# Products of the second layer's weights: from the end of the scatter to the waits behind feed-forward and query projections

## The chip, the cores and the metric

One core of one Trainium2 chip runs the whole program. The metric is the device time in microseconds of one execution. Inputs lie in the chip's memory when it starts. Inputs, weights and output are float32.

## The reference, cut to what matters

Two layers of a network on 1250 nodes with 512 features and 40,000 edges. Each layer adds a graph part and a mixing part to x and then a feed-forward part. The graph part of the first layer is attention over edges, and the second layer's is a graph convolution with two weights in a row:

```python
xn = _layernorm(x, axis=-1)
x = x + _L0_gnn_ref(xn, ...) + _L0_mix_ref(xn[None], ...)[0]
x = x + _L0_ffn_ref(_layernorm(x, axis=-1)[None], ...)[0]
xn = _layernorm(x, axis=-1)
x = x + _L1_gnn_ref(xn, edge_index, W_gcn, b_gcn, W_dense, b_dense) + _L1_mix_ref(xn[None], w_qkv, ..., w_q, w_k)[0]
x = x + _L1_ffn_ref(_layernorm(x, axis=-1)[None], w_q, keys, weight_down_embed, weight_up_embed)[0]

# L1_gnn:  agg = segment_sum(h[src] * norm) + b_gcn, h = embedding @ W_gcn;   return agg @ W_dense + b_dense
# L1_mix:  q, k, v from w_qkv;  alpha = softmax(einsum(q, w_q));  ...
# L1_ffn:  q = x @ w_q / sqrt(1 + eps);  h = einsum('bnd,bnhkd->bnhk', q, weights_down)
```

Three products of weights alone can be formed ahead of layer 2, and the kernel does: W_gcn W_dense with the bias b_gcn W_dense + b_dense + b_proj (`wgd`, `l1_bias`), the query weights times w_q by head (`aq`), and the last part's w_q times the 256 rows of weight_down that can be chosen (`wqd`).

## The kernel before, in words

The program is written by hand, engine by engine. The end of the kernel calls the stages of each engine one after the other (L2555 to L2610); the engines meet at the stage ends in `leave_stage` (L140: TensorE, ScalarE and VectorE each drain, count up `s_stage` and wait until all three have). Rows of nodes are worked on in 10 tiles of 125. SBUF is one tensor `arena`, in which each stage lays out its buffers by hand with `Space`, and PSUM is one tensor `banks` of 8 banks. A float32 matmul stands in the trace as two records.

Stages of layer 0, in order: edges, mix, gnn, att, ff, ffn, causal, expert. Beside edges, mix and gnn, GpSimd scatters the edges' weights into a table in memory of 1250 x 1250 cells with 9 numbers each (`edges_pool`, indirect DMAs at L503): 313 columns of 128 edges. A column is issued when the one before the last has landed (`s_scat`), and its values must have been summed by VectorE (`s_group`).

The stages that the change touches:

- `gnn_*` (L894 to L1101): attention's query, key and value projections, then the row maxima of the scores (L1071, reduced by VectorE at L961), then the shifts, transposed by TensorE (L1077) and copied by ScalarE (L1007, to `shiftT`). Behind these stands the folding of the weights: VectorE spreads `w_q` on a diagonal (L969 to L971), TensorE multiplies (`fold_part` L1083, biases L1091 and L1092), ScalarE copies the banks out (L1013, L1014), SyncE stores and loads the next pair of weights (L909), TensorE multiplies again (L1083, L1099), ScalarE copies (L1016, L1017) and SyncE stores (L914, L915). The handshake is one semaphore, `f_step`.
- `att_*` (L1168 on): attention over a table block of 125 x 250 cells at a time, 50 of them. SyncE first loads Wo, waits for the stage's end, loads W1, waits until all columns of the scatter have landed (`table_filled`, L507) and then loads three blocks, each in two transfers (L203, L204). ScalarE begins a block at L1277, and takes exponentials at L1280. A ring of three buffers holds the blocks.
- `ff_*`: feed-forward part. TensorE's matmuls at L1479 and in `project` (L189), VectorE adds the result at L1423 and takes statistics (L157) for the next layer norm.
- `ffn_*`: VectorE makes two layer norms in a row (L146 to L177); TensorE transposes z (L183), ScalarE copies it out as zT (L1581), TensorE projects on q, k and v (L189), VectorE copies (L1548). Then ScalarE squares (L1590), VectorE sums (L1552), a root (L1593) and norms follow, and TensorE transposes q and k (L183, copied at L1597).
- `l1_sp` loads the folded weights at 1904 us, when the expert stage starts (`s_fold`).

SyncE's queue is in the order of the program: a DMA that stands behind a wait goes out after it, whatever it is for.

```python
            sp.wait_ge(s_sum, TURNS)                  # L901, in gnn_sp
        def att_sp(sp):
            sp.dma_start(wo_g..., d["L0_gnn_Wo"])     # L1169
            sp.wait_ge(s_stage, 6)
            sp.dma_start(w1_most, ...)                # L1171
            table_filled(sp)
```

## Time and profile before

| what | before |
|---|---|
| runs, median (lowest to highest) | 2730.16 us (2728.12 to 2730.72), 3 runs |
| the profiled execution, its own time | 2739.05 us |
| its span, first to last instruction | 2737.3 us |
| mean granted TensorE clock | 0.911 |
| TensorE busy | 2327.8 us (85%) |
| VectorE busy | 1388.9 us (51%) |
| ScalarE busy | 737.6 us (27%) |
| GpSimd busy | 813.4 us (30%) |
| chain that ended last | TensorE 65%, VectorE 23%, ScalarE 5%, GpSimd 3%, issue 3%, DMA 1% |

How to read it: busy is the time in which an engine had an instruction of its own under way. The chain goes back from the last instruction, each step to what released it. PE is TensorE's matmul, PEld its weight loads, DVE is VectorE, ACT ScalarE, POOL GpSimd, SP SyncE, and a q behind a name is that engine's own queue. A granted clock of 1.00 is 2.4 GHz, 0.50 is 1.2 GHz. All starts are in us from the span's start.

### The profile page before, as it was taken

The page shows a single profiled execution, that of the slowest core. Times are in us where ns is not written, and L with a number is a line of the kernel's source. Part 1 is how long each engine was busy: PE and PEld are TensorE (multiplying, and loading weights), DVE is VectorE, ACT ScalarE, POOL GpSimd, SP SyncE. Part 2 cuts the span into 40 slices and gives each one's busy share as a digit, 9 for nine tenths or more (in the row PEclk, how much of TensorE's full clock was granted, in tenths as well). Part 3 has the DMA queues.
Part 4 walks back from the last instruction along what each step waited for, and adds up shares of the span by engine and source line. Part 5 has one row for each costly group of instructions (what it writes and reads, how often), then busy time and mean ns, then how long its engine had stood idle before and what let it go on. Part 6 is the DMA issues. An engine that isn't in the chain of part 4 may idle for free.

```text
span 2737.3 us, 30781 instructions
## 1 busy us (share of the span) xinstructions
PE 2327.8 (85%) x11164; PEld 1358.4 (50%) x11164; DVE 1388.9 (51%) x4120; ACT 737.6 (27%) x1583; POOL 813.4 (30%) x532
## 2 busy tenths in 40 slices
PE   1999895998968999988969588998999989988863
PEld 0455452443334444446634467777866733444431
DVE  4555666779906656641132533230122242499996
ACT  3111021220005444432211544442211110144432
POOL 2038887887836655530000000000000000012221
PEclk9997777998979999989989799996999999989977
DMA  9972222223248656640000200001100040000000
GB/s 347 418 283 3 3 3 18 4 4 41 3 116 207 169 156 167 164 139 1 1 0 0 93 1 1 1 1 65 60 1 1 1 111 16 0 1 9 10 8 11
DMA packets 90264, 180.59 MB, mean 66 GB/s; under 512 B 65109, under 2 KB 66070, under 8 KB 74135
## 3 DMA queue, kind: packets, MB, share of 16 engines
q1 hardware_dynamic: 44367, 176.77, 20.1%
q0 software_dynamic: 45072, 1.46, 5.1%
q8 instruction: 89, 1.46, 0.2%
q14 instruction: 62, 0.51, 0.1%
q10 hardware_dynamic: 674, 0.39, 0.1%
HBM read 110.27 MB, written 68.31 MB: 65 GB/s over the span
## 4 chain that ended last, share of the span: by engine, by line
PE 65%; DVE 23%; ACT 5%; POOL 3%; issue 3%; DMA 1%; SPq 0%; ACTq 0%; DVEq 0%; POOLq 0%
PE banks L189 19%; PE banks L1940 5%; PE banks L1967 5%; DVE arena L961 4%; PE banks L1769 4%; PE banks L1788 4%; PE banks L325 3%; PE banks L1479 3%; PE banks L1303 3%; PE banks L183 2%; PE banks L1316 2%; PE banks L1778 2%; PE banks L1803 2%; POOL arena L1260 2%; DVE arena L1228 1%
## 5 line engine op out<-in xcount | busy, mean ns | idle before, releaser
L189 PE MATMUL banks<-arena 128*125 128x512 f32 (+1 forms) x1280 | 602.9, 620 | 84.3 <-ACT arena L2444 74.9
L503 POOL DMA_INDIRECT edge_table<-arena x313 | 490.8, 1568 | 256.4 <-DMA edge_table<-arena 165.0
L189 PEld LDWEIGHTS banks<-arena 128*125 128x125 f32 x1280 | 245.6, 201 | 375.7 <-issue 279.5
L1228 DVE TENSOR_TENSOR arena<-banks,arena 125x500 f32<-125x500 f32 x200 | 208.6, 1051 | 180.0 <-ACT banks L1280 176.3
L1260 POOL TENSOR_TENSOR arena<-arena 125x500 f32<-125x500 f32 x180 | 222.5, 1245 | 173.1 <-DVE arena L1228 167.4
L2278 POOL MEMSET arena<- 128x1024 f32 x2 | 1.8, 951 | 675.0 <-DVEq L140 675.0
L183 PE MATMUL banks<-arena 125*128 125x125 f32 x600 | 101.5, 309 | 105.9 <-DVE arena L177 69.9
L1682 DVE CUSTOM_DVE_ANT_0 arena<-banks,arena 125x512 f32<-125x512 f32 (+8 forms) x144 | 74.9, 554 | 212.2 <-PE banks L1778 209.7
L1303 PE MATMUL banks<-arena 64*125 64x250 f32 x800 | 142.6, 434 | 36.9 <-DVE arena L1228 25.8
L1888 DVE SCALAR_TENSOR_TENSOR arena<-banks,arena 125x512 f32<-125x512 f32 x80 | 60.1, 751 | 203.7 <-PE banks L1967 203.7
L183 PEld LDWEIGHTS banks<-arena 125*128 125x128 f32 x600 | 76.6, 160 | 170.4 <-issue 94.2
L1280 ACT ACTIVATE banks<-banks 125x500 f32<-125x500 f32 x200 | 114.6, 573 | 172.5 <-PE banks L1306 172.1
L1940 PEld LDWEIGHTS banks<-arena 128*128 128x128 f32 x1280 | 144.5, 193 | 6.9 <-issue 6.8
L1940 PE MATMUL banks<-arena 128*128 128x125 f32 x1280 | 146.2, 276 | 0.0
L1967 PE MATMUL banks<-arena 128*125 128x512 f32 x320 | 139.1, 592 | 0.0
L1769 PE MATMUL banks<-arena 128*125 128x512 f32 (+10 forms) x288 | 117.9, 531 | 22.3 <-ACT arena L1719 22.3
L1316 PE MATMUL banks<-arena 125*64 125x250 f32 x800 | 130.8, 406 | 0.9 <-ACT arena L1266 0.7
L1071 PE MATMUL banks<-arena 64*125 64x512 f32 (+1 forms) x480 | 113.7, 578 | 6.0 <-DVE arena L961 4.7
L325 PE MATMUL banks<-arena 1*128 1x512 f32 x160 | 99.7, 706 | 20.5 <-DMA arena<-key_rows 12.8
L334 ACT ACTIVATE arena<-banks 128x512 f32<-128x512 f32 x80 | 47.8, 598 | 254.9 <-PE banks L325 249.7
L1303 PEld LDWEIGHTS banks<-arena 64*125 64x125 f32 x800 | 61.0, 187 | 109.9 <-DVE arena L1228 69.9
L1788 PE MATMUL banks<-arena 125*125 125x64 f32 x880 | 113.7, 281 | 1.5 <-ACT arena L1750 1.5
(314 smaller groups left out, 3621.1 us busy)
## 6 DMA issues: line engine op xcount, KB each, us to landing
edge_table<-arena SPq DMA_DIRECT2D x24, 2250.0 KB, 36.2
arena<-edge_table SPq DMA_DIRECT2D x50, 984.4 KB
arena<-L_ffn_W SPq DMA_DIRECT2D x4, 2048.0 KB, 8.4
arena<-edge_table SPq DMA_DIRECT2D x50, 114.3 KB
adjacency<-arena SPq DMA_DIRECT2D x50, 109.4 KB
arena<-adjacency SPq DMA_DIRECT2D x10, 546.9 KB
edge_table<-arena POOLq DMA_INDIRECT x313, 3.0
arena<-x SPq DMA_DIRECT2D x1, 2240.0 KB
```

The lines of the kernel that those rows point to most:

```text
L183: last = nc.tensor.transpose(dst[:, k, :], src[:, k * 128:(k + 1) * 128], ident[0:TP, 0:TP])
L189: last = nc.tensor.matmul(dst, xT[:, i, :], w[:, i, 0:n], start=(i == 0), stop=(i == k - 1))
L325: nc.tensor.matmul(line_bank(h), ones[p:p + 1, 0:EP], line[p:p + 1, :], start=True, stop=True).then_inc(s_wide, 1)
L503: pool.indirect_dma_start(d["table"], bass.IndirectOffsetOnAxis(ap=cell[0:EP, c:c + 1].bitcast(U32), axis=0), vals[0:EP, c * ROW:(c + 1) * ...
L1228: nc.vector.tensor_tensor(P_g[n % PRING][0:TP, :].rearrange("p (e n) -> p e n", e=2), two_scores(n), ring[(c * TILES + b) % RING][0:TP, :, ...
L1260: nc.gpsimd.tensor_tensor(total_p, P_g[(n - PAIRS) % PRING][0:TP, :] if b == 1 else total_p, P_g[n % PRING][0:TP, :], ALU.add).then_inc(a_ ...
L1303: nc.tensor.matmul(bank(at + e)[0:TP, 0:CHUNK], kT_g[64 * e:64 * e + 64, j, tok(b)], qT_g[64 * e:64 * e + 64, j, sources(c)], start=True, ...
L1316: last = nc.tensor.matmul(bank(j // 2)[64 * e:64 * e + 64, CHUNK * (j % 2):CHUNK * (j % 2 + 1)], V_g[0:TP, b, DH * (2 * j + e):DH * (2 * j ...
L1769: nc.tensor.matmul(bank(score_bank(s, j))[0:TP, 0:c1 - c0], qz_c[:, h, :], kT_f[:, h // 2, c0:c1], start=True, stop=True).then_inc(b_s, 1)
L1788: last = nc.tensor.matmul(bank(6)[0:TP, h * DH:(h + 1) * DH], pTc_v[0:TP, b, :], V_f[0:TP, b, h * DH:(h + 1) * DH], start=(b == 0), stop=( ...
L1940: last = nc.tensor.matmul(bank(2 + n % 3)[:, m * TP:(m + 1) * TP], w1_e[a // 2][:, k, (c % 8) * 128:(c % 8 + 1) * 128], yT[:, k, tok(t)], ...
L1967: last = nc.tensor.matmul(bank(5 + n % 3)[0:TP, :], hT_e[t % 2][:, 2 * e + c, :], w2_e[e // 4][:, 2 * (e % 4) + c, :], start=(c == 0), sto ...
```

## The change

The fold's work stays the same, instruction by instruction, apart from where it stands:

- The SyncE part, `fold_sp`, is called between `ffn_sp` and `expert_sp`. The first weights are loaded behind the projections' weights, at the start of feed-forward. Of the second pair `wqT` is loaded only when the first products have been stored (`s_fold` 32), since its buffer holds them.
- `fold_dve` is the last thing of `ff_dve`. Attention on VectorE no longer waits for `s_fold`.
- TensorE's first products (`fold_dense_pe`) are the first thing of `ffn_pe`, in banks 4 to 7 with the bias row in bank 3. ScalarE copies them out (`fold_dense_act`) behind its first zT, and TensorE waits for this before its second projection (bank 3).
- The second products (`fold_query_pe`, banks 5 to 7) stand behind the projections, and ScalarE copies them (`fold_query_act`) behind the root.
- The buffers lie at the end of the arena; products overwrite the weights that they were made from.

```diff
@@ -861,9 +861,6 @@
-        both_bias = kept_g.take(C)
-        wq_col, bg_col = kept_g.take(KC), kept_g.take(KC)
-        wq_diag = kept_g.take(KC * HEADS).rearrange("p (k h) -> p k h", h=HEADS)
@@ -875,11 +872,16 @@
-        fold = Space(3 * SLOT, 4 * SLOT)
-        left_w, right_w = chunks(fold.take(KC * C), C), chunks(fold.take(KC * C), C)
-        down_w = chunks(fold.take(KC * KEYS), KEYS)
-        fold = Space(BUF, BUF + 4616)
-        wgd_out, bias_out, aq_out, wqd_out = (fold.take(n) for n in (KC * C, C, KC * HEADS, KC * KEYS))
+        fold = Space(BUF + 4064, TOP)
+        both_bias = fold.take(C)
...
+        fold = Space(TOP - 2 * KC * C - KC * KEYS, TOP)
+        right_w, down_w = chunks(fold.take(KC * C), C), chunks(fold.take(KC * KEYS), KEYS)
+        left_w = chunks(fold.take(KC * C), C)
+        wgd_out, bias_out = right_w, both_bias
...
@@ -899,20 +901,6 @@
             sp.wait_ge(s_sum, TURNS)
-            for w, n in ((left_w, "L1_gnn_W_gcnT"), (right_w, "L1_gnn_W_dense"), (down_w, "L1_ffn_down")):
...
-            sp.wait_ge(f_step, 5)
-            sp.dma_start(d["aq"], aq_out).then_inc(s_fold, 16)
-            sp.dma_start(d["wqd"], wqd_out).then_inc(s_fold, 16)
@@ -1193,7 +1146,6 @@
         def att_dve(dve):
-            dve.wait_ge(s_fold, 16 * 4)
@@ -1426,6 +1378,7 @@
             dve.wait_ge(f_x, TILES)
+            fold_dve(dve)
             leave_stage(dve, "DVE")
@@ -1524,6 +1477,67 @@
+        def fold_sp(sp):
+            for w, n in ((left_w, "L1_gnn_W_gcnT"), (right_w, "L1_gnn_W_dense"), (down_w, "L1_ffn_down")):
+                sp.dma_start(w.rearrange("p k n -> p (k n)"), d[n]).then_inc(s_fw[0], 16)
...
+            sp.wait_ge(f_step, 2)
+            sp.dma_start(left_w.rearrange("p k n -> p (k n)"), d["L1_mix_WqT"]).then_inc(s_fw[1], 16)
+            sp.wait_ge(f_step, 3)
+            sp.dma_start(d["wgd"], wgd_out.rearrange("p k n -> p (k n)")).then_inc(s_fold, 16)
+            sp.dma_start(d["l1_bias"], bias_out[0:1, :]).then_inc(s_fold, 16)
+            sp.wait_ge(s_fold, 32)
+            sp.dma_start(right_w.rearrange("p k n -> p (k n)"), d["L1_ffn_wqT"]).then_inc(s_fw[1], 16)
+            sp.wait_ge(f_step, 5)
+            sp.dma_start(d["aq"], aq_out).then_inc(s_fold, 16)
+            sp.dma_start(d["wqd"], wqd_out).then_inc(s_fold, 16)
+
+        def fold_dve(dve):
+            dve.wait_ge(s_fw[0], 16 * 6)
+            link(dve, nc.vector.memset(wq_diag, 0.0))
...
+        def fold_dense_pe(pe):
+            pe.wait_ge(f_step, 1)
+            for m in range(KC):
+                fold_part(bank(4 + m), m, right_w)
+            for k in range(KC):
+                nc.tensor.matmul(bank(3)[0:1, :], bg_col[:, k:k + 1], right_w[:, k, :], start=(k == 0), stop=False)
...
+        def fold_dense_act(act):
+            act.wait_ge(f_step, 2)
+            for m in range(KC):
+                nc.scalar.activation(wgd_out[:, m, :], bank(4 + m), ACT.Copy)
+            nc.scalar.activation(bias_out[0:1, :], bank(3)[0:1, :], ACT.Copy).then_inc(f_step, 1)
+
+        def fold_query_pe(pe):
+            pe.wait_ge(s_fw[1], 32)
...
+        def fold_query_act(act):
+            act.wait_ge(f_step, 4)
...
@@ -1582,6 +1596,8 @@
                 last.then_inc(z_cols, 1)
+                if t == 0:
+                    fold_dense_act(act)
@@ -1591,6 +1607,7 @@
             nc.scalar.activation(sa[0:TP, :], sv[0:TP, :], ACT.Sqrt).then_inc(c_sr, 1)
+            fold_query_act(act)
@@ -1599,6 +1616,7 @@
         def ffn_pe(pe):
+            fold_dense_pe(pe)
             pe.wait_ge(s_wc, 16 * 8)
@@ -1613,10 +1631,13 @@
+                    if t == 0 and j == 1:
+                        pe.wait_ge(f_step, 3)
                     project(bank(2 + j)[0:TP, :], zT_c[t % 2], w).then_inc(c_proj, 1)
...
             pe.wait_ge(c_ev, 3 * TILES)
+            fold_query_pe(pe)
@@ -2563,6 +2584,7 @@
             ffn_sp(sp)
+            fold_sp(sp)
             expert_sp(sp)

```

How the order moves on SyncE, at the end of the gnn stage and the begin of attention (`fold_step` is `f_step`, `repeats_summed` is `s_sum`, `stage_left` is `s_stage`, `columns_scattered` is `s_scat`). Before:

```order
L909 DMA arena<-L_mix_WqT 128x2048 [waits fold_step]
L909 DMA arena<-L_ffn_wqT 128x2048
L911 DMA gcn_dense_weights<-arena 128x2048 [waits fold_step]
L912 DMA l_bias<-arena 1x512
L914 DMA global_query_weights<-arena 128x32 [waits fold_step]
L915 DMA expert_down_weights<-arena 128x1024
L1169 DMA arena<-L_gnn_Wo 128x2048
L1171 DMA arena<-L_gnn_W 128x3072 [waits stage_left]
L1172 DMA arena<-L_gnn_W 128x1024
L203 DMA arena<-edge_table 112x2250 [waits columns_scattered_1,columns_scattered_0]
L204 DMA arena<-edge_table 13x2250
L203 DMA arena<-edge_table 112x2250
```

The same place now, from the wait for `s_sum` on:

```order
L196 DMA arena<-L_gnn_ln_att_b 128x4
L1122 DMA arena<-L_gnn_Wo 128x2048 [waits repeats_summed]
L1124 DMA arena<-L_gnn_W 128x3072 [waits stage_left]
L1125 DMA arena<-L_gnn_W 128x1024
L203 DMA arena<-edge_table 112x2250 [waits columns_scattered_1,columns_scattered_0]
L204 DMA arena<-edge_table 13x2250
L203 DMA arena<-edge_table 112x2250
L204 DMA arena<-edge_table 13x2250
```

Wo's load follows the wait for `s_sum`, W1's the end of the stage, and no fold transfer is among them. They stand behind the projections' weights now:

```order
L196 DMA arena<-L_ffn_kn_g 128x1
L1482 DMA arena<-L_gnn_W_gcnT 128x2048
L1482 DMA arena<-L_gnn_W_dense 128x2048
L1482 DMA arena<-L_ffn_down 128x1024
L1483 DMA arena<-L_bias_rows 2x512
L1484 DMA arena<-L_mix_w_q 128x4
L1485 DMA arena<-L_gnn_b_gcn 128x4
L1487 DMA arena<-L_mix_WqT 128x2048 [waits fold_step]
L1489 DMA gcn_dense_weights<-arena 128x2048 [waits fold_step]
L1490 DMA l_bias<-arena 1x512
L1492 DMA arena<-L_ffn_wqT 128x2048 [waits folded_weights_stored]
L1494 DMA global_query_weights<-arena 128x32 [waits fold_step]
L1495 DMA expert_down_weights<-arena 128x1024
```

TensorE between feed-forward (last rows with 125x512 of it) and the projections, before:

```order
L189 MATMUL banks<-arena 125x512 x7
L183 MATMUL banks<-arena 128x125 [waits z_ready,ffn_qkv_weights_loaded,stage_left]
L183 MATMUL banks<-arena 128x125 x3
L189 MATMUL banks<-arena 125x512 [waits zT_ready]
L189 MATMUL banks<-arena 125x512 x3
L183 MATMUL banks<-arena 128x125 [waits z_ready]
L183 MATMUL banks<-arena 128x125 x3
L189 MATMUL banks<-arena 125x512 x8
```

And now:

```order
L189 MATMUL banks<-arena 125x512 x7
L1506 MATMUL banks<-arena 128x512 [waits fold_step,stage_left]
L1506 MATMUL banks<-arena 128x512 x15
L1515 MATMUL banks<-arena 1x512 x4
L1516 MATMUL banks<-arena 1x512
L183 MATMUL banks<-arena 128x125 [waits z_ready,ffn_qkv_weights_loaded]
L183 MATMUL banks<-arena 128x125 x3
L189 MATMUL banks<-arena 125x512 [waits zT_ready]
L189 MATMUL banks<-arena 125x512 x3
L183 MATMUL banks<-arena 128x125 [waits z_ready]
L183 MATMUL banks<-arena 128x125 x3
L189 MATMUL banks<-arena 125x512 [waits fold_step]
L189 MATMUL banks<-arena 125x512 x7
```

The 21 fold matmuls stand ahead of the first transposes, and the second projection has a wait for the copies.

## Rows read from the trace of the kernel before

**Rows 1.** Chain that ended last, 600 to 860 us: start us, us, what.

```profile
760.33 15.56 PE banks L1083 x32
...
780.76 8.73 DMA arena<-L_ffn_wqT
789.54 7.00 PE banks L1083 x32
796.53 9.50 PE banks L1099 x32
...
810.48 14.41 DMA arena<-edge_table
```

**Rows 2.** Timeline, SyncE queue: start us, us, engine line op out<-in.

```profile
780.39 0.33 SPq L909 DMA_DIRECT2D arena<-L_mix_WqT  x1
...
809.34 0.47 SPq L1172 DMA_DIRECT2D arena<-L_gnn_W  x1
809.92 0.50 SPq L203 DMA_DIRECT2D arena<-edge_table  x1
```

**Rows 3.** Timeline, ScalarE: in brackets idle time before and who ended it.

```profile
760.43 3.10 ACT L1007 ACTIVATE arena<-banks 8x500 bf16<-8x500 f32 x6 [128.37 <-PE banks L1077]
```

**Rows 4.** Timeline, GpSimd: columns of the scatter.

```profile
639.12 1.86 POOL L503 DMA_INDIRECT edge_table<-arena  x1 [2.02 <-DMA edge_table<-arena]
644.50 1.54 POOL L503 DMA_INDIRECT edge_table<-arena  x1 [3.52 <-DMA edge_table<-arena]
...
781.80 1.54 POOL L503 DMA_INDIRECT edge_table<-arena  x1 [0.30 <-issue]
790.60 1.54 POOL L503 DMA_INDIRECT edge_table<-arena  x1 [7.26 <-DMA edge_table<-arena]
```

**Rows 5.** One line, L503: time from a column's issue to its landing.

```profile
DMA to landing us min/median/max: 2.9/3.0/11.5
```

**Rows 6.** Chain that ended last, from feed-forward into the projections.

```profile
1380.62 0.60 DVE arena L157
...
1402.42 5.25 PE banks L189 x8
...
1408.10 10.30 PE banks L189 x24
```

**Rows 7.** Timeline, TensorE, first transposes of the projections.

```profile
1399.71 1.06 PE L183 MATMUL banks<-arena 125*128 125x125 f32 x4 [19.90 <-DVE arena L177]
```

**Rows 8.** Windows of 1 us: busy time by engine, then TensorE's granted clock, DMA share, GB/s.

```profile
1384.00:1385.00 1.00, 0.00 (x0) 0.00 (x0) 0.24 (x2) 0.62 (x2) 0.00 (x0) 1.00 0.00 0
1385.00:1386.00 1.00, 0.00 (x0) 0.00 (x0) 0.86 (x5) 0.00 (x0) 0.00 (x0) 0.55 0.00 0
1386.00:1387.00 1.00, 0.00 (x0) 0.00 (x0) 1.00 (x3) 0.00 (x0) 0.00 (x0) 0.50 0.00 0
```

**Rows 9.** Groups by line, 1511 to 1531 us: TensorE behind the projections.

```profile
L183 PE MATMUL banks<-arena 125*128 125x125 f32 x3 | 0.9, 424 | 19.3 <-DVE arena L1568 19.3
```

**Rows 10.** Timeline, SyncE queue, inside attention: one table block.

```profile
834.71 0.34 SPq L203 DMA_DIRECT2D arena<-edge_table  x1
```

**Rows 11.** Windows of 0.5 us, columns as in rows 8.

```profile
840.00:840.50 0.50, 0.50 (x6) 0.13 (x6) 0.00 (x0) 0.50 (x3) 0.46 (x1) 1.00 0.02 1
```

**Rows 12.** DMA issues by line, KB and median us to landing: W1's last part.

```profile
arena<-L_gnn_W SPq DMA_DIRECT2D x1, 512.0 KB, 10.9
```

**Rows 13.** Timeline, VectorE: the fold's memset and its last copy.

```profile
757.98 0.09 DVE L969 MEMSET arena<- 128x32 f32 x1
...
758.28 0.45 DVE L971 COPY arena<-arena 64x4 f32<-64x4 f32 x1
```

**Rows 14.** Timeline, ScalarE: copies of the first products.

```profile
780.39 2.06 ACT L1013 ACTIVATE arena<-banks 128x512 f32<-128x512 f32 x4 [16.87 <-PE banks L1092]
```

**Rows 15.** Timeline, ScalarE: the root behind the projections.

```profile
1526.60 0.34 ACT L1593 ACTIVATE arena<-arena 125x160 f32<-125x160 f32 x1 [1.03 <-DVE arena L1556]
```

**Rows 16.** Groups by line, 805 to 1210 us: ScalarE's first work on each table block.

```profile
L1277 ACT ACTIVATE arena<-arena 125x250 f32<-125x250 f32 x50 | 32.5, 650 | 17.8 <-DMA arena<-edge_table 17.8
```

More of the change, by code:

```diff
@@ L1010, in gnn_act @@
             last.then_inc(g_shift, 1)
-            act.wait_ge(f_step, 2)
-            for m in range(KC):
-                nc.scalar.activation(wgd_out[:, m * C:(m + 1) * C], bank(3 + m), ACT.Copy)
-            nc.scalar.activation(bias_out[0:1, :], bank(7)[0:1, :], ACT.Copy).then_inc(f_step, 1)
-            act.wait_ge(f_step, 4)
-            nc.scalar.activation(aq_out, bank(3)[:, 0:KC * HEADS], ACT.Copy)
-            nc.scalar.activation(wqd_out, banks[:, 4 * BANK:6 * BANK], ACT.Copy,
-                                 scale=1.0 / (1.0 + 1e-5) ** 0.5).then_inc(f_step, 1)
             leave_stage(act, "ACT")
@@ new lines, in fold_dve, with fold_part @@
+        def fold_dve(dve):
+            dve.wait_ge(s_fw[0], 16 * 6)
+            link(dve, nc.vector.memset(wq_diag, 0.0))
+            nc.vector.tensor_copy(wq_diag.rearrange("p k h -> p (k h)")[0:64, 0:KC * HEADS:10], wq_col[0:64, :])
+            nc.vector.tensor_copy(wq_diag.rearrange("p k h -> p (k h)")[64:128, 1:KC * HEADS:10],
+                                  wq_col[64:128, :]).then_inc(f_step, 1)
+        def fold_part(dst, m, right):
+            for k in range(KC):
+                last = nc.tensor.matmul(dst, left_w[:, k, m * 128:(m + 1) * 128], right[:, k, :],
+                                        start=(k == 0), stop=(k == KC - 1))
+            return last
@@ new lines, in fold_dense_pe @@
+        def fold_dense_pe(pe):
+            pe.wait_ge(f_step, 1)
+            for m in range(KC):
+                fold_part(bank(4 + m), m, right_w)
+            for k in range(KC):
+                nc.tensor.matmul(bank(3)[0:1, :], bg_col[:, k:k + 1], right_w[:, k, :], start=(k == 0), stop=False)
+            nc.tensor.matmul(bank(3)[0:1, :], ones[0:2, 0:1], both_bias[0:2, :], start=False, stop=True).then_inc(f_step, 1)
+        def fold_dense_act(act):
[3 more added lines that the diff above has]
+            nc.scalar.activation(bias_out[0:1, :], bank(3)[0:1, :], ACT.Copy).then_inc(f_step, 1)
@@ new lines, in fold_query_pe @@
+        def fold_query_pe(pe):
+            pe.wait_ge(s_fw[1], 32)
+            for m in range(KC):
+                fold_part(bank(5)[:, m * HEADS:(m + 1) * HEADS], m, wq_diag)
+            for m in range(KC):
+                for k in range(KC):
+                    last = nc.tensor.matmul(bank(6 + m // 2)[:, KEYS * (m % 2):KEYS * (m % 2 + 1)],
+                                            right_w[:, k, m * 128:(m + 1) * 128], down_w[:, k, :],
+                                            start=(k == 0), stop=(k == KC - 1))
+            last.then_inc(f_step, 1)
```

46 lines of the change are left out of this document (10 added, 36 removed).

## The prediction

> **What bounds the kernel now.** I read the chain of work that ended last first, around the place that the change empties. From 760.3 us it runs over TensorE's products of the second layer's weights, then the load of L1_ffn_wqT, then more products, and then 14.4 us of a table load, with which attention begins [rows 1]. So the folding stage itself bounds that stretch, and nothing of it is needed before layer 2. The question is what is next in line once it is gone. The SyncE queue says that: it issued L1_mix_WqT at 780.39, and the first W1 load and table block only at 809.3 and 809.9, after the last fold product [rows 2]. ScalarE, whose copies of the shifts are the last thing that the stage would have without the fold, started those at 760.43 and needed 3.1 us, so the stage could be left at about 763.8 [rows 3]. What is then late is the scatter on GpSimd: its 313th and last column was issued at 790.60, after a wait of 7.26 us for an earlier column's transfer [rows 4]. A column normally lands 3.0 us after its issue, and at worst 11.5 [rows 5]. The waits stand where SyncE moves megabytes: 2.02 and 3.52 us at 639 and 644, behind 2.5 MB of fold weights, and 7.26 us at 783 to 790, behind 2 MB of loads and 1 MB of stores. Elsewhere a column follows its predecessor after 0.30 us.
>
> Then I read the two places that take the work in. Between feed-forward and query projections TensorE stands idle for 19.9 us, and then it does its first four matmuls of the projections (8 records) in 5.25 us, where later ones take 10.30 us for 24 [rows 6, 7]: its granted clock had fallen from 1.00 to 0.55 and then 0.50 by 1386 [rows 8], that is from 2.4 to 1.2 GHz, after some 5 us without work. Behind the projections it stands idle for 19.3 us more [rows 9].
>
> **The change, part by part.**
>
> *The end of the scatter.* Three transfers change on SyncE while columns are under way. (a) At 635 us the queue issues W_gcnT, W_dense and down, 2.5 MB, and now only the 1 MB of L0_gnn_Wo. The stall of 2.02 + 3.52 - 2 x 0.30 = 4.94 us shrinks in proportion to 40%, so 3.0 us are saved. The ends are 0 (the stall comes from any load) and 4.94. (b) At about 763.8 the 2 MB of L0_gnn_W1 now start, beside the scatter: 4.94 x 2/2.5 = 4.0 us of new stall. The ends are 0 and 6.96, the stall of the larger burst. (c) The burst at 780 goes: 7.26 - 0.30 = 6.96 us saved [rows 4]. The last column is then issued at 790.60 - 3.0 + 4.0 - 6.96 = 784.6 and lands at 787.6.
>
> One rule of the Trainium skill speaks of (a) to (c). "DMA: Bandwidth & Descriptors", section "Queues, rings and completion order", says that a DMA engine goes round the queues that have work, a packet from each at a time. By that a column waits for a packet and not for megabytes, and (b) would cost nothing. The trace speaks against it with its 7.26 us.
>
> *The first table block.* It is now issued when the last column has landed, and nothing is ahead of it. The nearest row is a single block in the middle of attention: issued at 834.71, with the DMA engines quiet from 840.0, which is 5.3 us [rows 10, 11]. The other end is what block 0 took before, from 809.92 to 824.97 = 15.1 us, with 3 MB of Wo and W1 ahead and two blocks behind; of these W1's last part landed 10.9 us after its issue, at 820.2, and block 0 only 4.7 us later [rows 2, 12]. I take 6.5 us: the single block and a little for the two blocks queued behind it. Attention then begins at 787.6 + 6.5 = 794.1 instead of 824.97. This is **30.9 us** sooner. From there on it runs as before.
>
> *Between feed-forward and projections.* VectorE gets the memset and two copies of the diagonal weights, on the path, since its layer norm follows: from 757.98 to 758.73 = **0.75 us** [rows 13]. TensorE gets 16 + 4 + 1 matmuls, 42 records. At full clock 512 columns take 10.30 / 24 = 0.43 us a record [rows 6], so 18.0 us. It can begin when VectorE has left the stage, at 1380.62 + 0.60 + 0.75 = 1382.0, and the first transpose of the projections is ready at 1399.71 + 0.75 = 1400.5. That is 18.4 us of cover for 18.0 us of work. It just fits, and if the cover were gone each further microsecond would be late. The clock should stay up, because the gap before the fold is 2.2 us and the clock fell only after 5. So transposes and first projection find it high: four transposes take about 0.65 instead of 1.08 us, and eight records 3.44 instead of 5.25, together 2.2 us won. ScalarE copies five banks out behind its first zT, 4 x 512 columns in 2.06 us and a fifth of 0.5, 2.6 us in all [rows 14]; TensorE needs those banks only after 3.44 + 0.43 us of other work, so this costs nothing. The sum here is 0.75 - 2.2 = **-1.5 us**. The loads that this needs, 2.5 MB behind the projections' weights, are issued at the start of feed-forward, over 150 us before they are waited for.
>
> The second rule is on the clock. "TensorE: Matmul & The Clock Gate", section "HAM oscillation — how this bites in real kernels", says that work broken up by waits may drop to the lower clock again each time. It would put the gaps around the fold at 1.2 GHz and take the 2.2 us away. Which it is, no row of before shows for this pattern.
>
> *Behind the projections.* 32 more matmuls took 7.00 + 9.50 = 16.5 us before, part of it at half clock [rows 1]. They lie in the 19.3 us in which VectorE and ScalarE form the norms [rows 9]. ScalarE's two copies, together some 1.2 us by that same rate, come behind its root at 1526.60 [rows 15] and before the first transposed tile that it waits for, some 4 us later. The chain of transfers in between (WqT in, products out, wqT in) has over 100 us. This costs nothing. If the cover failed, only what exceeds 19.3 us would show. The stores of the products are needed in layer 2 only.
>
> *Sum.* -30.9 - 1.5 = -32.4 us. The profiled execution took 2739.05 us, so 2706.7 of its kind. The median of the runs, 2730.16, lies 8.9 us lower, and the same step from there gives **2698 us** (2697.8).
>
> **The rivals.**
>
> *Table blocks stay slow.* The 15.1 us of block 0 came from the three blocks that share the engines and not from the 3 MB ahead. For it: all three are issued within 3 us, and nothing says that the first of them is served first. Against it: 4.7 us after W1 sufficed [rows 2, 12]. Attention begins 8.6 us later than I say, so 2706.4.
>
> *Columns are hardly disturbed by W1.* That is the mechanism of a fair share between the queues, under which (b) costs nothing. The last column lands 4.0 us earlier: 2693.8, and with the 5.3 us of a single block 2692.6. For it: W1 is two transfers, where the burst at 635 was six, of which any may have been the one in the way. Against it: the stall at 783 to 790, behind two loads and a store [rows 4]. It is the round-robin of the rule cited above.
>
> *The fold outlives its cover.* The clock falls before or in the fold, and 42 records at twice 0.43 us take 36 us: 17.7 us late. Then the gain of 2.2 us is gone too, and -30.9 + 0.75 + 17.7 = -12.5 gives 2717.7. Against it: the short gap, and the matmuls stand without a wait among them.
>
> *Attention becomes bound by its table loads.* This is the one that ends slower. Attention begins with block 0 alone in memory, and blocks 1 and 2 still on their way, so it runs closer behind its loads. Before, ScalarE waited for a table block 17.8 us in all 50, all of it at the first [rows 16]. If the loads set the pace and each of the 50 blocks took over 32.4 / 50 = 0.65 us longer, all would be lost; at 0.8 us it is 40 - 32.4 = 7.6 us slower, 2737.8. Against it: a single block took 5.3 us, and the engines were then quiet.
>
> *Nothing moves.* Something else than the fold holds attention until 825. The chain and the queue's order leave little room for that: 2730.
>
> **How the numbers follow.** Forecast 0.62; slow table blocks 0.14; undisturbed columns 0.12; fold outlives its cover 0.06; attention bound by its loads 0.03; nothing moves 0.03. The forecast's own spread is 2694 to 2703, by the ends of (a), (b) and of the 2.2 us. The range takes in the cases on both sides of it, down to 2690 (no stall by W1 and the whole 4.94 us at 639 saved) and up to 2708. A measurement of this kernel can tell some 0.2%, 5.5 us, from no change. Faster by more than that are the first four cases and most of a spread around them, 0.94; same 0.03; slower 0.03.
>
> **What would show it.** In the profile after, the last GpSimd column should be issued near 784.6 (780 to 788) with stalls at 637 of 1 to 3 us and new ones of about 4 us just behind 764; the first exponential's chain should start near 794. The chain should show GpSimd's issues and no product between 760 and 790. The 42 fold records should start some 2 us behind the last feed-forward matmul and take 18 us, the granted clock should stay 1.00 until the projections, and ScalarE's copies should keep no one. The query products should end before the transposes. I am wrong if the last column comes at 790 again, if block 0 needs over 9 us, or if TensorE shows the fold still running when the first transposed rows are ready. A chain that passes through table loads later in attention would mean the rival that ends slower.

## The result, and the profile after

| what | before | after |
|---|---|---|
| runs in one job, median (lowest to highest) | 2729.32 us (2728.12 to 2730.72), 4 runs | 2712.84 us (2708.07 to 2715.86), 4 runs |
| ratio of after to before | | 0.9938, interval 0.9921 to 0.9955 |
| profiled execution / its span | 2739.05 / 2737.3 us | 2713.70 / 2712.0 us |
| mean granted TensorE clock | 0.911 | 0.914 |

Faster by 0.6%, or 16.5 us. The forecast was 2698 us and its range ended at 2708. In a second job the kernel after, unaltered, had 2708.69 us, at a ratio of 0.9915 (0.9902 to 0.9928).

The two profiled executions lie 25.3 us apart in their spans. The chain of work that ended last, in the profile after, from 600 to 860 us (start us, us, what), answers to [rows 1]:

```profile
629.51 5.94 DMA edge_table<-arena
635.72 2.98 POOL edge_table L503
...
758.02 8.57 DMA edge_table<-arena
...
791.10 2.94 DMA edge_table<-arena
794.44 6.59 DMA arena<-edge_table
```

There is no product between 760 and 790 any more; the chain is the scatter, column by column, and then the first table block. Its columns in the timeline of GpSimd answer to [rows 4], and the SyncE queue to [rows 2]:

```profile
631.42 1.87 POOL L503 DMA_INDIRECT edge_table<-arena  x1 [0.36 <-DVE arena L425]
635.72 2.98 POOL L503 DMA_INDIRECT edge_table<-arena  x1 [2.44 <-DMA edge_table<-arena]
639.01 1.67 POOL L503 DMA_INDIRECT edge_table<-arena  x1 [0.30 <-issue]
...
766.86 1.54 POOL L503 DMA_INDIRECT edge_table<-arena  x1 [5.46 <-DMA edge_table<-arena]
...
791.10 1.54 POOL L503 DMA_INDIRECT edge_table<-arena  x1 [0.42 <-issue]
```

```profile
630.36 0.33 SPq L1122 DMA_DIRECT2D arena<-L_gnn_Wo  x1
758.90 0.33 SPq L1124 DMA_DIRECT2D arena<-L_gnn_W  x1
...
794.06 0.34 SPq L203 DMA_DIRECT2D arena<-edge_table  x1
794.44 0.41 SPq L204 DMA_DIRECT2D arena<-edge_table  x1
```

The stall behind 780 is gone, and the one of W1 is there, just behind 759, as forecast. But the last column is issued at 791.10, where the forecast had 784.6. ScalarE starts its first block 10.0 us behind that (first line). Its copy of the last block starts at 1160.32 (second line); before, it started at 1185.69 (L1285):

```profile
801.11 0.65 ACT L1229 ACTIVATE arena<-arena 125x250 f32<-125x250 f32 x1 [42.27 <-DMA arena<-edge_table]
...
1160.32 0.38 ACT L1237 ACTIVATE arena<-banks 125x250 f32<-125x250 f32 x1 [0.41 <-PE banks L1280]
```

Between feed-forward and projections TensorE's timeline now reads as follows; it answers to [rows 6, 7]. The last two are the first products of q, k, v, and what follows on them:

```profile
1356.37 13.97 PE L1506 MATMUL banks<-arena 128*128 128x512 f32 x32 [1.97 <-DVEq L140]
1370.27 3.59 PE L1515 MATMUL banks<-arena 128*1 128x512 f32 x8
1373.80 1.01 PE L1516 MATMUL banks<-arena 2*1 2x512 f32 x2
1374.74 0.65 PE L183 MATMUL banks<-arena 125*128 125x125 f32 x4
1377.03 5.21 PE L189 MATMUL banks<-arena 128*125 128x512 f32 x8 [1.65 <-ACT arena L1595]
...
1382.51 7.89 PE L189 MATMUL banks<-arena 128*125 128x512 f32 x18
```

The 42 records of the fold run at full clock, take 18.4 us and end just when the first transposes can begin. The windows behind it (columns as in [rows 8]) show the granted clock falling from 1.00 to 0.50, thus from 2.4 to 1.2 GHz, in a gap of 1.65 us behind the transposes:

```profile
1375.00:1376.00 1.00, 0.39 (x4) 0.15 (x2) 0.55 (x1) 0.51 (x2) 0.00 (x0) 1.00 0.41 49
1376.00:1377.00 1.00, 0.00 (x0) 0.00 (x0) 0.00 (x0) 1.00 (x4) 0.00 (x0) 0.85 0.58 164
1377.00:1378.00 1.00, 0.97 (x1) 0.50 (x2) 0.00 (x0) 1.00 (x3) 0.00 (x0) 0.50 1.00 426
```

Behind the projections the query products lie in the wait, with 4.34 us to spare [rows 9]:

```profile
1490.74 9.83 PE L1530 MATMUL banks<-arena 128*128 128x256 f32 x32
1504.91 5.27 PE L183 MATMUL banks<-arena 125*128 125x125 f32 x25 [4.34 <-DVE arena L1582]
```

### The profile page after: what moved, and what is told of

Its sections match the earlier page's. It is cut to its first block, busy times and chain, and to the rows that moved or that the text cites. A ratio compares the mean times of both kernels' runs of the same rounds, so it can differ in the third digit from the quotient of the medians.

```text
span 2712.0 us, 30781 instructions
## 1 busy us (share of the span) xinstructions
PE 2316.4 (85%) x11164; PEld 1349.5 (50%) x11164; DVE 1390.1 (51%) x4120; ACT 737.7 (27%) x1583; POOL 818.3 (30%) x532
## 4 chain that ended last, share of the span: by engine, by line
PE 47%; POOL 18%; DVE 14%; issue 6%; DMA 5%; SPq 5%; ACT 4%; DVEq 0%; ACTq 0%; POOLq 0%
POOL edge_table L503 15%; PE banks L189 9%; PE banks L1961 5%; DMA edge_table<-arena 5%; PE banks L1988 5%; SPq L293 4%; PE banks L1790 4%; PE banks L1809 4%; PE banks L1432 3%; PE banks L1255 3%; PE banks L1268 2%; PE banks L1799 2%; PE banks L1824 2%; POOL arena L1212 2%; DVE arena L1180 1%
## 5 line engine op out<-in xcount | busy, mean ns | idle before, releaser
L503 POOL DMA_INDIRECT edge_table<-arena x313 | 495.7, 1584 | 252.3 <-DMA edge_table<-arena 161.3
```

The lines of the kernel that those rows point to most:

```text
L503: pool.indirect_dma_start(d["table"], bass.IndirectOffsetOnAxis(ap=cell[0:EP, c:c + 1].bitcast(U32), axis=0), vals[0:EP, c * ROW:(c + 1) * ...
```

## The experiments

All profiles are read by four lengths: when the last column is issued; from there to ScalarE's first block; attention, from that to ScalarE's copy of the last block; and the rest of the span.

| profile | last column | to first block | attention | rest | span |
|---|---|---|---|---|---|
| before | 790.60 | 34.37 | 360.72 | 1551.6 | 2737.3 |
| before_again | 787.68 | 32.37 | 358.65 | 1551.6 | 2730.3 |
| before_no_adds | 790.64 | 21.22 | 359.28 | 1553.6 | 2724.7 |
| after | 791.10 | 10.01 | 359.21 | 1551.7 | 2712.0 |
| a_again | 785.94 | 10.18 | 359.24 | 1551.5 | 2706.9 |
| more_load | 787.21 | 10.11 | 359.10 | 1554.9 | 2711.3 |
| adds_double | 782.65 | 10.29 | 363.02 | 1551.8 | 2707.8 |
| adds_late | 785.31 | 10.04 | 359.93 | 1550.7 | 2706.0 |
| w1_late | 776.61 | 10.30 | 363.51 | 1551.6 | 2702.0 |
| w1_wo_late | 782.70 | 9.98 | 373.03 | 1548.7 | 2714.4 |
| block0_alone | 785.04 | 9.77 | 361.55 | 1552.0 | 2708.4 |
| fill_gap | 784.67 | 9.88 | 359.49 | 1549.5 | 2703.5 |
| w1_pieces | 780.51 | 10.18 | 361.25 | 1551.8 | 2703.7 |
| best | 776.02 | 9.87 | 363.13 | 1551.8 | 2700.8 |

**The kernel after once more (a_again).**

> The changed kernel once more, unaltered. Theory (the scatter now sets when attention begins, so its stalls, which fall differently in each execution, show in the time): runs spread over some 8 us as before (2708 to 2716), the last column is issued between 786 and 794 us, and its time differs from this profile's 2713.7 by about as much as the last column differs from 791.1. Rival (the profile was a chance one and something else spreads the runs): last column within 1 us of 791.1, time elsewhere by several us.

It took 2708.69 us (2705.85 to 2710.46). The last column came 5.16 us sooner than in the first profile, and the span is 5.1 us shorter; the three other lengths agree within 0.2 us. So the kernel after follows its last column one for one. W1's stall is the same again (5.63 us at 761.76).

**W1 out of the scatter (w1_late), and Wo too (w1_wo_late).**

```diff
-            sp.dma_start(w1_most, ...)      # and w1_last, in att_sp ahead of table_filled
...
+                if i == 5:                  # behind table block 8 in attention
+                    sp.dma_start(w1_most, ...)      # w1_wo_late: Wo ahead of it, too
```

> The changed kernel with the 2 MB of L0_gnn_W1 loaded behind the sixth table block, no longer beside the scatter. Theory (megabytes on SyncE's queue hold up the scatter's columns, and the scatter bounds): no 5 us stall at about 760 us, last column some 5 us earlier (786), and 5 us less in all, 2708. Rival (queues share fairly, the stall at 766.9 was chance): last column unchanged within 2 us, 2713.

> As the run before, and the 1 MB of L0_gnn_Wo moved behind the sixth table block too. Theory: the stall of 3.6 us at 632 to 636 goes as well, last column 8 to 9 us earlier than in the changed kernel (782 to 783), 2704. Rival (one megabyte is too little to hold a column): as w1_late.

Without W1 no column waits behind 754 us; the first fence is w1_late, columns 301 to 313. In attention ScalarE then waits for a table block, which it does nowhere in the kernel after but at the first one (second fence, w1_late):

```profile
754.36 1.54 POOL L503 DMA_INDIRECT edge_table<-arena  x1 [0.30 <-issue]
...
776.61 1.54 POOL L503 DMA_INDIRECT edge_table<-arena  x1 [0.39 <-issue]
```

```profile
845.76 0.64 ACT L1230 ACTIVATE arena<-arena 125x250 f32<-125x250 f32 x1 [2.56 <-DMA arena<-edge_table]
```

Attention takes 4.3 us more, and the median is 2708.53 us (ratio 0.9924, 0.9907 to 0.994): the same as a_again. With Wo there too attention takes 373.0 us, 2710.94 us (ratio 0.9921, 0.9908 to 0.9933). W1's stall is W1's own: shown, since the four kernels without W1 beside the scatter have no such wait. What I had not expected stands in w1_wo_late. With Wo gone, the stall at 635 was still there. Its GpSimd and VectorE rows, and the window (columns as in [rows 8]) in which only 6 GB/s move:

```profile
631.48 6.11 DVE L934 TENSOR_TENSOR arena<-arena 125x512 f32<-125x512 f32 x10
632.03 1.55 POOL L503 DMA_INDIRECT edge_table<-arena  x1 [0.30 <-issue]
635.50 3.50 POOL L503 DMA_INDIRECT edge_table<-arena  x1 [1.91 <-DMA edge_table<-arena]
639.30 1.66 POOL L503 DMA_INDIRECT edge_table<-arena  x1 [0.30 <-issue]
```

```profile
630.00:635.00 5.00, 3.92 (x16) 1.92 (x18) 4.83 (x13) 0.00 (x0) 3.09 (x2) 0.50 0.28 6
```

Two columns are 3.58 us late here (start to start, beyond the usual 1.845 us), beside VectorE's ten additions of the output bias (L934 after, L946 before). These lay beside SyncE's burst in before too. The lateness has two parts. The issue at 635.50 itself took GpSimd 3.50 us instead of 1.54, and ahead of it GpSimd waited 1.91 us for a transfer. For that wait the additions are not the only candidate: at 633.2, in the same microseconds, stands a transfer of 16 KB on queue 8, of the kind that the profile calls instruction. This is the queue list of w1_wo_late from 632 to 635 us:

```profile
q0 software_dynamic: 288, 0.01, 30.9%
q8 instruction: 1, 0.02, 2.0%
```

The small pauses of the scatter go with these transfers as well. In the 14 profiles, from 250 to 755 us and leaving out the places of loads and additions and column 297 (0.7 to 0.9 us late in each), 58 columns were late by 0.7 to 1.6 us. 57 of them were issued 2.0 to 3.1 us behind the start of a 16 KB transfer of this kind. Of the 2841 columns that were on time (late by under 0.1 us), 48 were. No run moved these transfers, so that they hold the columns up is argued from this coincidence. Every profile has one beside the additions, too.

**A megabyte more (more_load).**

```diff
             sp.dma_start(w1_last, ...)
+            sp.dma_start(ring[0]..., d["L0_gnn_Wo"])      # 1 MB into a free buffer
+            sp.wait_ge(s_wo_g, 32)                       # ahead of the first table block
```

> The changed kernel with one megabyte more loaded beside the scatter at the stage's end, a copy of L0_gnn_Wo into a ring buffer that is still free (nothing reads it). Theory (a stall grows with the megabytes, 2.6 us each): stall of 7 to 8 us in place of 5.2, last column near 793.5, 2715 to 2716. Rival (a fixed stall for any burst): stall stays at 5.2, 2713.

```profile
760.65 1.54 POOL L503 DMA_INDIRECT edge_table<-arena  x1 [4.59 <-DMA edge_table<-arena]
762.97 1.54 POOL L503 DMA_INDIRECT edge_table<-arena  x1 [0.78 <-DMA edge_table<-arena]
```

The median was 2712.27 us (2705.18 to 2714.53). 3 MB cost the scatter 4.8 us in this one profile. The 2 MB of W1 cost 5.2 (after), 5.3 (a_again), 4.2 (adds_double), 5.0 (adds_late), 5.5 (block0_alone) and 4.8 us (fill_gap). From 2 to 3 MB the stall doesn't grow. It is no fixed sum either. In each of the 14 profiles SyncE loads four biases of 256 KB each at some 430 us (a_again from 429.02 on), and one column behind them is late by only 1.6 to 2.3 us:

```profile
434.14 1.54 POOL L503 DMA_INDIRECT edge_table<-arena  x1 [1.90 <-DMA edge_table<-arena]
```

The burst that the change removed, 2 MB in and 1 MB out, cost 7.0, 7.6 and 7.4 us in before, before_again and before_no_adds, each with a 16 KB instruction transfer beside it, which W1's stall did not have.

**Which of the two makes the stall at 637: loads or additions.**

```diff
 # before_no_adds (from before; it leaves the output bias out), and adds_late (from after)
-            for t in range(TILES):
-                nc.vector.tensor_tensor(XN[0:TP, t, :], XN[0:TP, t, :], bo_g[0:TP, :], ALU.add)
 # adds_late, in att_dve, its bias loaded into another place
+                if c == 0 and j == 2:
+                    nc.vector.tensor_tensor(XN[0:TP, b, :], XN[0:TP, b, :], bo_k[0:TP, :], ALU.add)
 # adds_double (from after): a wait for the end of each of the ten, and ten more behind them
-                nc.vector.tensor_tensor(XN[0:TP, t, :], XN[0:TP, t, :], bo_g[0:TP, :], ALU.add)
+                link(dve, nc.vector.tensor_tensor(XN[0:TP, t, :], XN[0:TP, t, :], bo_g[0:TP, :], ALU.add))
+            for t in range(TILES):
+                link(dve, nc.vector.tensor_tensor(z_g[0:TP, :], XN[0:TP, t, :], bo_g[0:TP, :], ALU.add))
```

> The kernel before without VectorE's ten additions of the output bias to x (it leaves them out), which lie exactly beside the stall of the scatter at 637 us, at the same moment as SyncE's 2.5 MB. Theory A (VectorE's two-operand additions in SBUF keep GpSimd from writing its descriptors; 3.6 us of the 4.9 are theirs): the stall there shrinks to 1 to 2 us. Theory B (the prediction: the megabytes make the whole stall): it stays 4.5 to 5.5 us. The time moves by no more than the stall and the 6 us of additions taken off VectorE's chain in front of the maxima.

> The kernel after with the ten additions taken out of the scatter's time: each stands in attention, one in each of the first ten table blocks, behind a product of that block. Wo's megabyte stays where it is. Theory A: no column near 630 to 640 us waits over 1 us, the scatter gains 3 to 3.6 us less what Wo's megabyte costs by itself, and VectorE leaves the stage 6 us sooner, so W1 is issued sooner. Attention takes 359.2 us as in the kernel after, or up to 3 us more if the ten additions are not hidden. Time 2704 to 2710 against 2708 to 2713 of the kernel after. Theory B: 3 to 4 us of stall remain at the load, and nothing is gained.

> The kernel after with ten further additions of the same size on VectorE behind the ten, their results thrown away, each with a wait for its end. The megabyte of Wo is loaded as before. Theory A (the additions make the stall): two to three columns are held up, in all 6 to 8 us instead of 3.6. Theory B (the load makes it): 3.6 us as now, over when the load is in. The stage's end moves by 6 to 7 us with the additions in either case, so the stall of W1 starts later too.

```profile
627.10 1.62 POOL L503 DMA_INDIRECT edge_table<-arena  x1 [0.34 <-issue]
635.36 1.54 POOL L503 DMA_INDIRECT edge_table<-arena  x1 [6.64 <-DMA edge_table<-arena]
```

These are before_no_adds. The stall is 6.4 us with no addition beside it: theory A falls for the kernel before. In adds_late one column waits 4.21 us at 636.57 with no addition beside it either, 4.0 us late. So neither load nor additions are needed for a stall, and the two don't add up:

| beside the columns at 625 to 650 us, besides 16 KB of instructions in each | columns late by |
|---|---|
| 256 KB of bias (best) | 1.5 us |
| ten additions (w1_wo_late) | 3.6 us |
| 1 MB and 256 KB of bias (adds_late) | 4.0 us |
| 1 MB and the additions (after, a_again, more_load, w1_late, block0_alone, fill_gap, w1_pieces) | 3.9, 3.9, 4.0, 4.0, 4.0, 4.4, 3.2 us |
| 2.5 MB (before_no_adds) | 6.4 us |
| 2.5 MB and the additions (before, before_again) | 5.2, 6.1 us |

Some 1.5 us of each may thus be neither of the two. What is the additions' own is the long issue: with the ten back to back, GpSimd took 2.7 to 3.8 us for one issue in seven of ten profiles. In the four others (before_no_adds, adds_late, best and adds_double) no issue here took over 1.91 us.

The edit of adds_double does more than its expectation says: it puts a wait behind each of the first ten additions too. Its first ten additions and Wo cost 2.0 us in one column and 0.3 to 0.7 us in those around it, some 3 us in all. Beside the second ten, columns took 1.87 us instead of 1.54 and none waited. That speaks against A as forecast (6 to 8 us). It also suggests that additions hold GpSimd up badly only back to back, but no run separates the waits between them from the missing load and instruction transfer.

adds_late had a median of 2707.34 us (ratio 0.9912, 0.9897 to 0.9926), the same as a_again; the one run of adds_double 2709.50.

**The kernel before once more (before_again).**

> The kernel before, unchanged, for a second profile. The scatter's columns were 3 to 5 us later or earlier from one profile to the next of the kernels after, from pauses of 1 to 2.4 us at changing places. Theory (the 2739 us of the first profile were the slow end of that spread): the last column is issued between 775 and 790 us and the profiled time is 2722 to 2738, moving with it one for one. The stretch from the last column to the first block's start is 34 us in both, the attention 360.7 us, and what is behind it 1551.6 us, all within 1 us. Rival (the change itself cost the other 5 us somewhere behind attention): the last column comes at 790 again and the time is near 2739. The stall at about 637 us should be 4 to 5.5 us again in either case.

It took 2732.06 us, 7.0 us less than the first profile of before. Its chain, against [rows 1]:

```profile
753.22 15.60 PE banks L1083 x32
...
773.69 8.51 DMA arena<-L_ffn_wqT
782.25 7.00 PE banks L1083 x32
789.24 9.63 PE banks L1099 x32
...
803.33 16.64 DMA arena<-edge_table
```

The fold starts 7.1 us sooner, while the last column came only 2.9 us sooner. Of the 7.1 us, 4.9 reach the first table block (820.05 instead of 824.97), since its load takes 2.2 us longer here; another 2.1 us of the difference in time are in attention. The 7.1 us arise far ahead, in the mixing part. VectorE's 12th and 16th sum of a turn (L425) come at 268.43 and 366.74 in before (first fence), and at 269.25 and 359.42 here (second):

```profile
268.43 0.23 DVE L425 TENSOR_TENSOR arena<-arena 128x72 f32<-128x72 f32 x1
...
366.74 0.23 DVE L425 TENSOR_TENSOR arena<-arena 128x72 f32<-128x72 f32 x1
```

```profile
269.25 0.23 DVE L425 TENSOR_TENSOR arena<-arena 128x72 f32<-128x72 f32 x1
...
359.42 0.23 DVE L425 TENSOR_TENSOR arena<-arena 128x72 f32<-128x72 f32 x1
```

TensorE's granted clock was 0.80 from 250 to 270 us in the one and 0.97 in the other. That alone doesn't set it: in a_again it was 0.74 there, and the 16th sum came at 360.27. What costs the 7 us stays open. My rival in this expectation falls, and so does half of the theory: the slow end of the spread did not sit in the scatter, but in the TensorE and VectorE chain beside it.

Which of the two chains bounds each kernel can now be read from the table. before_no_adds issued its second weights (L909) 8.7 us sooner than before_again, had its last column at 790.64, 3.0 us later than before_again, and was 5.6 us shorter: before follows the stage. adds_double issued W1 at 762.07, 8.4 us later than a_again, had its last column 3.3 us sooner, and its first block too: after follows the scatter.

**The first block alone (block0_alone).**

```diff
                 load_block(i)
+                if i == 0:
+                    sp.wait_ge(s_tab[0], 32)
```

> The kernel after, but table blocks 1 and 2 are issued only when block 0 has landed. In the kernel after block 0 is issued with two more right behind it and ScalarE starts 10.0 to 10.3 us after the last column's issue in seven profiles. Theory (it shares the engines with the two behind it): alone it lands after some 5.3 us, as the single block in attention did, so ScalarE starts 8.3 to 8.8 us after the last column; block 1 is in before it is wanted, at 9.3 us. Rival (its own size or the last column's landing sets it): 10.0 to 10.3 us stay. Time lower by 1.5 us or the same, read from the stretch alone.

```profile
787.95 0.34 SPq L203 DMA_DIRECT2D arena<-edge_table  x1
...
794.75 0.31 SPq L203 DMA_DIRECT2D arena<-edge_table  x1
794.81 0.64 ACT L1231 ACTIVATE arena<-arena 125x250 f32<-125x250 f32 x1 [32.74 <-DMA arena<-edge_table]
```

Block 0 takes 6.9 us from its first issue to ScalarE's start, alone as well as with two behind it (7.05 in after). From the last column it is 9.77 us, 0.1 under the shortest of the others. The theory falls: the blocks behind it slow it by no more than 0.2 us.

**TensorE's clock in the gap (fill_gap).**

```diff
+            for k in range(2):
+                nc.tensor.matmul(bank(3)[0:1, :], bg_col[:, k:k + 1], right_w[:, k, :], start=True, stop=True)
             for k in range(KC):
```

> The kernel after with two more bias matmuls of 512 columns (four records, 1.7 us) in the fold between feed-forward and projections, their results thrown away. They fill TensorE's gap of 1.65 us between the fold and the first transposes. Theory (the clock fell because of that gap): the granted clock stays at 1.00 through 1380 us, the first four matmuls of the projections take 3.4 to 3.6 us instead of 5.2, and the place is 1.7 to 1.9 us shorter, or 1.6 if the transposes come 0.1 late. Rival (it falls for the waits behind the transposes, or later): 5.2 us again and a place of 28.0 us.

```profile
1371.70 0.65 PE L183 MATMUL banks<-arena 125*128 125x125 f32 x4
1373.99 3.70 PE L189 MATMUL banks<-arena 128*125 128x512 f32 x8 [1.65 <-ACT arena L1597]
```

The expectation had misread the gap. TensorE goes from fold to transposes without one; the 1.65 us come behind the transposes, where ScalarE copies the first zT, and they were there in this run as well. The clock stayed up all the same: 3.70 instead of 5.21 us. Nothing shows that as an effect of the edit. The nine other profiles of kernels with the unchanged fold besides after have the same gap, and in two of them, w1_wo_late (1383.43) and block0_alone (1374.99), it was 3.70 us too; in the others 5.2 to 5.3. What differs is the clock's past: in the eight it had last fallen 92 us before it fell here, in w1_wo_late, block0_alone and fill_gap 76, 22 and 77 us before this place. The place is 28.20 us (from VectorE's last feed-forward addition to the products behind the second transposes) against 28.00: the 1.7 us added were paid for, and 1.5 came back. One run says no more.

**Loads in small pieces (w1_pieces), and all together (best).**

```diff
 # w1_pieces: behind table blocks, one piece of 128 KB each
+                if 3 <= i < 19:
+                    k, part = divmod(i - 3, 4)
+                    at = slice(part * 4 * HID // 16, (part + 1) * 4 * HID // 16)
+                    sp.dma_start(w1_g[k][:, at], d["L0_gnn_W1"][:, k * HID + at.start:k * HID + at.stop])
 # best: Wo likewise at i = 1 to 8, W1 at 9 to 24, and the edit of adds_late
```

> The kernel after with W1 loaded in 16 pieces of 128 KB, one behind each of the table blocks 3 to 18 in attention, instead of 2 MB beside the scatter. Theory: no column waits near 760 us, as when all of W1 went behind the sixth block, so 5 us of stall are gone; and attention stays at 359 to 360 us, where W1 in one piece made it 363.5. Time 5 us under the kernel after, 2703 to 2708. Rival (the table's loads leave no room for any other): attention 363 us or more, and the time is that of the kernel after.

> The kernel after with no transfer and no additions beside the scatter behind 630 us: Wo in 8 pieces behind table blocks 1 to 8, W1 in 16 pieces behind blocks 9 to 24, and the ten additions in attention. Theory: neither stall is left (3.9 us near 635 and 5.2 us near 760 less), the last column is issued at 770 to 777, attention takes 360 us. Time 8 to 9 us under the kernel after, 2700 to 2704. Rival (attention pays for the loads and the additions): attention 363 to 368 us and 2704 to 2710.

w1_pieces: 2704.43 us (2696.38 to 2706.65), ratio 0.9893 (0.9873 to 0.9913). best: **2700.99 us** (2699.59 to 2702.51), ratio 0.9885 (0.9866 to 0.9904). Each of its five runs is below all nine of the kernel after, but those were in other jobs, and the interval of the ratio just touches that of a_again (0.9902 to 0.9928). In best's scatter, neither stall is left, though its edit keeps a bias load of 256 KB at 636.06; what stands near 640 are two waits of 1.01 and 0.71 us:

```profile
639.13 1.90 POOL L503 DMA_INDIRECT edge_table<-arena  x1 [1.01 <-DMA edge_table<-arena]
641.74 1.55 POOL L503 DMA_INDIRECT edge_table<-arena  x1 [0.71 <-DMA edge_table<-arena]
...
776.02 1.54 POOL L503 DMA_INDIRECT edge_table<-arena  x1 [0.38 <-issue]
```

Attention is 363.1 us, and my rival had said 363 to 368. But 4.15 of it is one block of 11.36 us where a_again has 7.21, with TensorE granted 0.50 from 945 to 948 us. adds_double had that event too (11.32 us, at the same block), with nothing loaded or added in attention, and its attention was 363.02 us. Against that profile the pieces cost 0.1 us. The event stands in before, before_no_adds and fill_gap at the same block as well, so it is not the pieces' doing. That they are free rests on such pairs of profiles, not on the medians.

## Why the prediction was wrong

**What bounds the kernel now.** Right, and it named what is late next: the scatter. The profile of after is bound by it all the way from 600 to 794 us.

**The end of the scatter.** Forecast 784.6, measured 791.1 and 785.9. (c) held: the 6.96 us went. (b) is the term that was undersized: 5.2 us in the first profile and 4.2 to 5.5 in six, instead of 4.0. (a) was oversized: "shrinks in proportion to 40%" saved 1.3 us (5.2 to 3.9) and not 3.0. A stall is not proportional to its megabytes: 2 MB cost 4.2 to 5.5 us, 3 MB 4.8. The step also took VectorE's ten additions and the 16 KB of instructions for no part of it, and without Wo these two still cost 3.6 us. The last 3.4 us had built up by column 232, ahead of all three transfers. The prediction put them at nothing with "Elsewhere a column follows its predecessor after 0.30 us", and that misreads its own profile: nine more columns of before, from 250 to 755 us, were late by 0.7 to 1.8 us. Which columns are hit changes from one profile to the next: column 232 was 3.4 us later in after and 1.9 us sooner in a_again than in before. Between after and a_again, delays over 0.5 us make 4.6 of these 5.3 us, nine of them in the one and four in the other. Between before and after they make 0.9 of the 3.4 us, and the rest are the first columns and smaller delays.

The rival *Columns are hardly disturbed by W1*, a fair share between the queues, falls: W1's stall is there with the load and gone without it. From the round-robin in "DMA: Bandwidth & Descriptors" of the Trainium skill, section "Queues, rings and completion order", I had concluded that a column would wait for a packet and (b) would cost nothing. The trace disagrees with that conclusion by 5.2 us; whether a share by packets can make such a stall, no run here shows. A page that I had not weighed, "SBUF — State Buffer" of the Trainium skill, section "SBUF: two separate sides", says that while VectorE holds the port pair that it shares with GpSimd, GpSimd can't write its descriptors, and a transfer looks blocked. For operations with two inputs in SBUF it says so only against a GpSimd operation that reads SBUF. The issue of 3.50 us instead of 1.54 in w1_wo_late would agree with it; no run shows that the ports are the cause.

**The first table block.** 6.5 forecast, 7.05 measured: right within 0.5 us. *Table blocks stay slow* falls, and block0_alone shows that the two behind it make no more than 0.2 us of it.

**From there on it runs as before.** 359.2 against 360.7 us, 1.5 us less; before_again had 358.7. *Attention becomes bound by its table loads* did not occur; but w1_late shows how near it is, with 2.56 us of waiting for a block once 2 MB are loaded beside it.

**Between feed-forward and projections.** 0.0 us instead of -1.5 (28.02 us before, 28.00 after, measured as in fill_gap). The fold took 18.4 us and not 18.0, and it still fit the cover, so *The fold outlives its cover* falls. The memset and copies cost 0.4 us and not 0.75, and the four transposes gained 0.4 as said. The 1.8 us of the first projection did not come: "the gap before the fold is 2.2 us and the clock fell only after 5" was the failed step, since it fell in another gap, of 1.65 us, behind the transposes (1.00, 0.85, 0.50). The rule that I had cited, in "TensorE: Matmul & The Clock Gate" of the Trainium skill, section "HAM oscillation — how this bites in real kernels", says that waits between stretches of work can bring the lower clock back each time, with an example of longer waits. Of ten profiles with this fold unchanged, the clock fell at this gap in eight and stood in two.

**Behind the projections.** 0, as forecast.

**Sum.** In the frame of the profiled execution I said 2706.7; a profile gave 2713.7 and another 2708.7. Of the 7.0 us in the first, 6.5 are the last column, 0.5 the block and 1.5 the clock, less 1.5 in attention.

**From the profile to the median.** "The same step from there gives 2698" is the step that cost most, 8.9 of the 14.8 us by which I missed. It holds if what makes one execution slower than the median is still in the kernel afterwards. Here most of it was not. The first profile of before took 7.0 us more than before_again: 4.9 us of that are in the start of the first table block, from the 7.1 us that arose ahead of 367 us on the TensorE and VectorE chain, and 2.1 in attention. That chain bounded before up to its table load. After, the stage is left over 30 us ahead of the last column, so it bounds no more there, and its excess was already part of the 30.9 us that I had taken off. Subtracting it again counted it twice. An estimate from these rows: with the first block of before_again, 820.05 - 794.1 = 26.0 us, the forecast of -1.5 us and its time of 2732.06, the same working gives 2704.6 in the frame of a profiled execution. That is 4.1 us under a_again: 1.3 in the last column, 0.7 in the block, 1.4 in the clock and the rest behind attention, 0.6 in attention.

What stays open: why a stall hardly grows from 2 to 3 MB, how a 16 KB instruction transfer holds a column up, what costs the 7 us in the mixing part, and what lets the clock stand in two of ten.

## What to carry to other kernels

When a change takes the bounding chain away, work out the new time from the start of the chain that takes over, in absolute terms, and take neither the old chain's excess nor its luck over to the median; a second profile of before would have shown which of them carries it. A queue of small dependent transfers is held up by large ones beside it, here by 1.6 to 7.6 us and not in proportion to their size, so it can pay to move such loads, in pieces, to where they meet work with slack. Before putting a stall down to the loads beside it, look at what VectorE does and at what else the DMA queues carry in those microseconds.

## What the runs showed of the hardware that I had not expected

- One issue of an indirect transfer took GpSimd 2.7 to 3.8 us instead of 1.54 beside ten back-to-back VectorE additions with both inputs in SBUF (6.11 us), in seven of ten profiles. With a wait behind each addition it was 1.91 us at most.
- Of 58 small pauses of the scatter (0.7 to 1.6 us), 57 ended 2.0 to 3.1 us behind the start of a 16 KB instruction transfer, and of 2841 columns on time 48 did. It is a coincidence in the traces and not tested.
- The additions cost the scatter 3.6 us without the 1 MB load, the load 4.0 without the additions, and both together 3.2 to 4.4, each with 16 KB of instructions beside them.
- Behind the same 1.65 us gap the granted clock fell to 0.50 in eight of ten profiles and stood at 1.00 in two: 5.2 to 5.3 or 3.7 us for eight records.
